# Message sums of layer 1 in fours instead of twos, 8.25 instead of 8 one-hot products per step, and no picks for the last two groups

## What is computed

```python
# layer 0: messages of an MLP over (x[dst], x[src], edge_attr_32), summed per destination
h = relu(concat([x[dst], x[src], edge_attr_32]) @ W1 + b1)
x = layernorm(x + segment_sum(h @ W2 + b2, dst))
# layer 1: x[src] + edge_attr_48, relu, summed per destination
m = relu(x[src] + edge_attr_48)
x = layernorm(x + (1 + eps) * x + segment_sum(m, dst))
```

## Time and profile before

| | us |
|---|---|
| three runs: median (lowest to highest) | 4189.63 (4186.67 to 4202.98) |
| the profiled execution's own time | 4189.34 |
| its span | 4187.5 |

### The profile page before, as it was taken

The page is one execution under the profiler, slowest core; times in us unless marked ns, Lnnn a source line. Parts: engine busy times, 40 slices in busy tenths (PEclk is TensorE's granted clock), DMA queues, the critical chain, the costliest instruction groups (busy, mean ns, idle before and its releaser), DMA issues.

```text
span 4187.5 us, 58888 instructions
## 1 busy us (share of the span) xinstructions
PE 3720.4 (89%) x21330; PEld 2934.2 (70%) x21330; DVE 2151.9 (51%) x4308; ACT 658.0 (16%) x1275; POOL 2554.6 (61%) x2692
## 2 busy tenths in 40 slices
PE   4699899998899999999997888998888898898998
PEld 3476667776676776677776777777677777777777
DVE  2343333443443443434444666666666666666665
ACT  1222222222222222222221000000000000001111
POOL 6666666666666666655563666666666666666664
PEclk9698989989989988989997999999999999999988
DMA  5222222222222222222221222222222222222222
GB/s 105 33 34 35 34 34 35 34 34 36 34 35 35 34 36 34 36 32 37 40 37 33 48 48 49 48 48 47 48 46 52 46 48 49 48 49 49 50 51 45
DMA packets 408204, 178.79 MB, mean 43 GB/s; under 512 B 279085, under 2 KB 407075, under 8 KB 407811
## 3 DMA queue, kind: packets, MB, share of 16 engines
q0 software_dynamic: 86016, 66.23, 11.5%
q1 hardware_dynamic: 319778, 108.26, 11.3%
q10 hardware_dynamic: 2114, 0.49, 0.1%
HBM read 169.74 MB, written 5.00 MB: 42 GB/s over the span
## 4 chain that ended last, share of the span: by engine, by line
PE 44%; another core or an unknown queue 23%; DVE 19%; issue 12%; DVEq 1%; SPq 0%; ACT 0%; DMA 0%
PE ps_h L869 9%; PE ps_t L869 9%; PE ps_early L869 7%; DVE picked L1087 6%; PE ps_out L776 5%; PE ps_h L827 5%; PE ps_as L768 4%; DVE at_place L1078 4%; DVE edge L997 3%; PE ps_nodes L879 2%; PE ps_t L794 2%; DVE acc L1011 2%; DVE pre L1111 1%; DVE msg L1014 1%
## 5 line engine op out<-in xcount | busy, mean ns | idle before, releaser
L554 POOL DMA_INDIRECT edge<-x,resid_sb x1430 | 1359.8, 951 | 850.2 <-issue 392.7
L554 POOL DMA_INDIRECT edge<-x_dram,resid_sb x1258 | 1194.6, 950 | 751.9 <-issue 380.3
L869 PE MATMUL ps_t<-x_parts,at_place 125*128 125x480 f32 x3040 | 787.5, 410 | 73.7 <-issue 72.2
L869 PE MATMUL ps_early<-x_parts,at_place 125*128 125x480 f32 x2680 | 742.2, 426 | 36.8 <-DVE edge L997 24.2
L869 PE MATMUL ps_h<-x_parts,at_place 125*128 125x480 f32 x3080 | 746.3, 396 | 23.0 <-issue 17.7
L869 PEld LDWEIGHTS ps_t<-x_parts,at_place 125*128 125x128 f32 x3040 | 607.3, 204 | 211.0 <-issue 110.8
L1078 DVE TENSOR_TENSOR at_place<-place_row,ps_out 125x1280 fp32r<-125x1280 f32 x440 | 651.5, 1481 | 194.8 <-remote 177.6
L869 PEld LDWEIGHTS ps_early<-x_parts,at_place 125*128 125x128 f32 x2680 | 530.1, 200 | 242.2 <-issue 133.9
L869 PEld LDWEIGHTS ps_h<-x_parts,at_place 125*128 125x128 f32 x3080 | 595.2, 196 | 134.7 <-issue 32.3
L1033 DVE COPY w_edge<-ps_as 48x128 f32<-48x128 f32 x391 | 112.4, 287 | 788.1 <-remote 712.5
L776 PE MATMUL ps_out<-w_sb,hT 128*128 128x48 f32 x3128 | 456.7, 299 | 60.0 <-issue 59.3
(11 more groups left out here) (64 smaller groups left out, 1766.4 us busy)
## 6 DMA issues: line engine op xcount, KB each, us to landing
e_sb<-e SPq DMA_DIRECT2D x196, 192.0 KB
place_row<-rows_dram SPq DMA_DIRECT2D x440, 62.5 KB
edge<-e SPq DMA_DIRECT2D x196, 128.0 KB
edge<-x,resid_sb POOLq DMA_INDIRECT x1430
edge<-x_dram,resid_sb POOLq DMA_INDIRECT x1258
x_win<-xT SPq DMA_DIRECT2D x391, 9.0 KB
acc<-xT SPq DMA_DIRECT2D x10, 234.4 KB
feats<-x SPq DMA_DIRECT2D x10, 234.4 KB
```

The lines of the kernel that those rows point to most:

```text
L554: pool.indirect_dma_start(out=cols, out_offset=None, in_=rows_of, in_offset=bass.IndirectOffsetOnAxis(ap=index, axis=0)).then_inc(done, 16)
L869: last = nc.tensor.matmul(banks[q % len(banks)], lhsT=at_place[:, q % PLACED, c, :], rhs=x1_parts[:, c, part, :], start=(c == 0 and part = ...
```

## The change

- TensorE and VectorE do the sums of four groups together, in the first step of each iteration (`u == 0`), rather than of two in every other step. `ps_s` has four regions, in the same bank.
- VectorE adds nothing before all four are there: the wait for `S["seg"]` is for the last of the four, so that it doesn't read a bank into which TensorE writes.
- Two waits are added for slots that the later sums keep longer: ACT writes `msg` of a group only when the group four back has been summed, and VectorE writes `pre1` in the first step of an iteration only when `msg` of the group four back is done.
- The rates of products are 8.25 and 7.25, `find_places` stands up to 0.2 steps nearer to its pick (1.7 rather than 1.9 steps ahead at least), and the last two groups have no pick: 314 picks instead of 306.

```diff
@@ plan @@
-                picks.append((select + 1, math.floor(begun - 1.9), select))
+                picks.append((select + 1, math.floor(begun - 1.7), select))
@@ module @@
-PLAN, PRODUCTS = plan([(s, 10 if s < 0 else 8 if s < UNROLL * NORM_ITER else 7) for s in range(-AHEAD, GROUPS)], GROUPS - 1)
+PLAN, PRODUCTS = plan([(s, 10 if s < 0 else 8.25 if s < UNROLL * NORM_ITER else 7.25) for s in range(-AHEAD, GROUPS)], GROUPS - 3)
@@ build @@
-        ps_as = pb("ps_as", [P, H + WIN])
+        ps_as = pb("ps_as", [P, H + 2 * WIN])
         ps_a = [ps_as[0:WIN, 0:H], ps_as[TALL:TALL + WIN, 0:H]]
-        ps_s = [ps_as[0:D, H:H + WIN], ps_as[TALL:TALL + D, H:H + WIN]]
+        ps_s = [ps_as[first:first + D, H + k * WIN:H + (k + 1) * WIN] for k in range(2) for first in (0, TALL)]
@@ scalar, steps1 @@
                     wait_group(act, S1["sum"], i, u)
+                    wait_for(act, S1["seg"], (i - 1) * UNROLL + u)
@@ tensor, sum_messages @@
-                if S is S1 and g % 2 == 0:
+                if S is S1 and g % UNROLL == 0:
                     wait_for(pe, S["acc"], g - 1)
-                    last = nc.tensor.matmul(ps_s[g % 2], lhsT=msg[:, g % UNROLL, t, :], rhs=edge[:, g % RING, t, 0:WIN],
+                    last = nc.tensor.matmul(ps_s[g % (2 if S is S0 else UNROLL)], lhsT=msg[:, g % UNROLL, t, :], rhs=edge[:, g % RING, t, 0:WIN],
@@ tensor, steps1 @@
-                if u % 2 == 0:
-                    for back in (2, 1):
+                if u == 0:
+                    for back in range(UNROLL, 0, -1):
@@ vector, accumulate @@
-                    wait_for(dve, S["seg"], g)
-                nc.vector.tensor_tensor(acc[0:D, bass.ds(first, WIN)], acc[0:D, bass.ds(first, WIN)], ps_s[g % 2], ALU.add).then_inc(S["acc"], 1)
+                    wait_for(dve, S["seg"], min(g - g % UNROLL + UNROLL, GROUPS) - 1)
+                nc.vector.tensor_tensor(acc[0:D, bass.ds(first, WIN)], acc[0:D, bass.ds(first, WIN)], ps_s[g % (2 if S is S0 else UNROLL)], ALU.add).then_inc(S["acc"], 1)
@@ vector, steps1 @@
+                    if u == 0:
+                        wait_for(dve, S1["msg"], g - UNROLL)
...
-                if u % 2 == 0:
-                    for back in (2, 1):
+                if u == 0:
+                    for back in range(UNROLL, 0, -1):
```

## The result

| | us |
|---|---|
| kernel before, median (lowest to highest, 4 runs) | 4192.3 (4186.67 to 4202.98) |
| changed kernel, median (lowest to highest, 4 runs) | 4250.95 (4245.4 to 4261.25) |
| ratio, 95% interval | 1.0135, 1.0116 to 1.0153 |
| the changed kernel's profiled execution, its span | 4247.7, 4245.9 |

Forecast were 4163 us, with a range up to 4205. Of all the runs told of here one, of one group per step with the change's rates, fell in a slower state of the chip (4295.9 us at a granted clock of 0.75), and its ratio leaves that run out.

A forecast was written before the change was run, and what follows sets the result against it. TensorE in layer 1 was taken as the bound, in a loop over VectorE and ACT with late words of sums. Terms 35.6 - 14 - 52 - 10 + 12 + 2 = -26 against 4189.3 gave 4163 us, range 4115 to 4205.

The forecast's parts named there:

- waits before sums: TensorE's 104.4 us idle before sums in layer 1: half goes, -52 us, between -90 and 0.
- the prediction's own sign of being wrong: Wrong if layer 1's idle time before sums doesn't fall, or if gathers are waited for before `pre`.
- the wait moves into the products: Rival: TensorE, stopped less before sums, runs into unnamed stops before products; 4187 us, chance 0.24.
- the loop with the mean wait of 3.4 us: TensorE's sums over VectorE and ACT to its next sums: put at 14 us, against four steps' 19.5.
- Products, +35.6 us: Eight more picks in layer 1 put 160 matmuls of 0.223 us on TensorE's path, counted in full: +35.6 us.
- products for nothing: Rival: the added matmuls fall into gaps TensorE has anyway; 4127 us, chance 0.05.
- Hand-overs, -14 us: TensorE's changes between products and sums: 97 fewer at 0.14 us each, -14 us, between -20 and 0.
- Clock, -10 us: Layer 1's granted clock of 0.95 loses 77 us; an eighth comes back with fewer stops: -10 us.
- Places, +12 us: Finds in first steps end later, so TensorE's picks wait for `at_place`: +12 us, between 0 and +66.
- late places: Rival: late words of sums make picks wait up to +66 us; 4253 us at worst, chance 0.14.
- The end, +2 us: Layer 1's tail from last product to last adding: about 7 us where it was 4.5, +2 us.
- no change: Rival case of 4187 us, chance 0.24; its sign was "issue" idle time before products over 110 us.

The follow-up runs named there:

- one group per step with the change's rates: Kernel before, each step summing one group two steps back, with the change's product rates and finds: 4172.4 us, ratio 0.9948, with stops.
- Twos one step later: Kernel before, each block summing the groups two and three steps back instead of one and two: 4190.8 us (0.9992) with stops, 3481.7 us (0.9987) without.
- rates alone: Kernel before with the change's three edits of the plan, sums still in twos: 4175.3 us (0.9958) with stops, 3486.0 and 3486.8 us without.
- fours alone: Changed kernel with the products of before (rates 8 and 7, finds 1.9 steps ahead): 4259.0 us (1.0155) with stops, 3486.9 and 3486.0 us without.
- block spread among products: Changed kernel with two products between each group's sums and the next on TensorE: 4201.6 us (1.0033) with stops, 3585.9 and 3586.3 us without.

## Why the prediction was wrong

The step that failed is the one on **waits before sums**: "What takes their place on TensorE's queue is products, which wait for nothing of VectorE's but `at_place`." It gave the change -52 us, and the prediction's own sign of being wrong came true: idle time before sums didn't fall but rose from 104.4 to 174.4 us. The mechanism named there was right and even underrated: the waits for `msg` fell from 64.6 to 0.3 us, not by half. But time was not won with them. Twos one step later show it by itself: 65 us of waits away, ratio 0.9992. And the block of four was priced at 1.3 us. Undisturbed it is 1.15 us, but only 24 of 98 blocks are free of stops, and all together take 3.7 us on average. I had the 129 us without a named releaser before me and took them as they were, to be counted in place, rather than asked what they would do to the longest run of short instructions that the change makes. The rival "the wait moves into the products" had the right kind of thing, in the wrong place and at half its size: the stops moved into the blocks, where idle time without a name rose by 134 us (39.4 to 173.1), while before products it fell by 53 (89.9 to 36.9). One sum in this step is wrong too: the loop with the mean wait of 3.4 us makes 16.2 us, not 14. Either is under the 19.5 of four steps, so nothing hangs on it.

Term by term, against what was measured:

- **Products, +35.6 us.** Each matmul still takes its time (eight in 1.84 us from 2507.31, up to the next record at 2509.15), but rates alone came out 17 us faster, not 36 slower. In the condition with stops TensorE's idle time in layer 1 fell from 204 to 173 us with them, and the waits for `msg` nearly halved (34.6 us). Without stops they cost 2 to 3 us of the 36. No profile of the kernel before was kept there, but two versions with its products wait for gathers there (224 us with fours alone, 255 with twos one step later), so TensorE had room as well. That is what the rival "products for nothing" said, which had 0.05, and the rule of the Trainium skill ("Trainium Kernel Development and Optimization", section Performance Expectations) on the weight loads' share: 71% busy, room left. The trace agrees here, though there is less room than the other 29%: rates alone without stops have TensorE busy in 1591.2 of 1593 us of layer 1 with the weight loads at 84%. Which of the three edits of the plan brings the 17 us was not tried.
- **Hand-overs, -14 us.** 0.14 each was too low. Two clean blocks of two hold the products 1.42 us and one of four 1.15, so the hold alone gives 0.27; 118 us for 294 in the condition without stops are 0.40 each, by which 97 fewer would be -39 us. The fours gained 18.5 us there (3486.8 to 3468.2): TensorE's busy time fell by 25 us, and its idle time rose by 8, since the gathers are now nearly the bound. Fours alone, with 8 gathers more and 160 matmuls fewer, gained nothing there.
- **Clock, -10 us.** Wrong in sign: 0.95 to 0.93, and 0.87 to 0.81 in the last stretch. Over the versions the clock of layer 1 falls as TensorE's idle time grows: 1.00 with 2 us idle, 0.96 with 110, 0.90 with 231 and with 265.
- **Places, +12 us.** There, at about half its size: 5.4 us of matmuls and 8.3 of weight loads now wait for `at_place`, where it was 2.1 of weight loads. The forecast's rival "late places", the one that ended slower, is not what made it slower.
- **The end, +2 us.** The last product ends at 4226.71, the last adding at 4234.46: 7.8 us where it was 4.5, +3.2.
- **Which stretch.** I gave none of the loss or gain to the last stretch by itself. It carries 38 of 62 us. There the norm's ten short matmuls stand directly behind the block, so the run is 42 records where it was 26. With the block spread among products, the same stretch takes 350 us instead of 389 (3841.1 to 4191.0), and took 351 before.

The test that I had named for "no change" and for the forecast was the wrong one to tell them apart: idle time before products did fall, from 92.1 to 43.8 us, and idle time before sums rose without `msg` in it.

## What to carry to other kernels

Idle time that the profile puts down to nothing is a part of the bound like any other: before a change that takes waits away, ask whether it is the engine's own and where it will settle. Here long runs of short matmuls were where it settled, so where such idle time is in the trace, try long instructions between them before gathering more. Where it was absent, gathering them paid, until another engine's gathers were the bound. And a change of this size can turn its sign with the condition in which it is measured, so always time it beside the kernel before.

## What the runs showed of the hardware

**Two conditions of TensorE.** The kernel before takes 4192 us in one and 3484 in the other, and instructions of other engines are as long as before. Rates alone without stops, the gathers and a bank's picks (from its page):

```profile
L554 POOL DMA_INDIRECT edge<-x_dram,resid_sb x1250 | 1187.0, 950 | 449.7 <-issue 342.4
L869 PE MATMUL ps_h<-x_parts,at_place 125*128 125x480 f32 x3160 | 733.8, 386 | 4.6 <-DVE x_parts L1168 4.6
```

A gather is 950 ns long, as in the earlier trace rows. A matmul's mean is 386 ns against 395 to 410 there, and the granted clock 0.98 against 0.91. Rates alone take 684 us more of profiled time with stops (4157 against 3473 us up to the end of layer 1): 357 are idle time of TensorE, and 327 are longer busy time, at a granted clock of 0.89 instead of 0.97 in layer 0 and 0.95 instead of 1.00 in layer 1. How much of the busy time is the clock's was not worked out. Where the condition comes from, no run shows.

**Stops.** They come in bites 0.7 us apart, in products as in sums. They don't go with the number of signals that tell of thirds (1.0026 with two thirds of them gone). That long runs of short matmuls collect them is shown by the fours alone (a stop in 67 of 98 blocks) and spread (in 40 of 386); what the engine lacks in them is open. The rows suggest a reason, which is argued and not shown. In the block at 2583.17 a bite has one to six records. Six sums in a row take some 0.2 us, while three products fill 0.67 (0.22 each), so bites of a few records cost long matmuls little and short ones much. That its instructions, all written out, reach it late is a rival that no run tried.

**The late word.** The signal of a finished sum came 5.6 to 7.1 us after its recorded end in the earlier trace rows, and 3.7 us after it in the block above (4211.27 to 4215.00). It belongs to the same condition: with rates alone and no stops, VectorE's adding waited on nothing remote, and nine in ten of these signals came 15 ns after the recorded end. Whether the word is late or the recorded end early, the profile can't tell.

**Hand-overs.** Going from picks to sums and back costs TensorE 0.40 us of busy time once more (118 us for 294), in the condition without stops.
